# The recurrence's scaled input: one VectorE operation in place of two on GpSimd

## The chip, the cores and the metric

The kernel runs on one core of a Trainium2 chip. The metric is the device time of one execution, in microseconds (us). Five engines work side by side: TensorE (PE; its weight loads are listed apart, as PEld), VectorE (DVE), ScalarE (ACT), GpSimd (POOL) and SyncE (SP, which here only issues DMAs). Each takes its instructions in the order in which the program gives them, and an instruction that waits for a semaphore holds up everything behind it on its engine.

## The reference

The program is a decoder of two layers over 8 sequences of 256 tokens, 256 wide: windowed attention, cross-attention, experts; then a gated linear recurrence, cross-attention, a binarized feed-forward. Each sublayer is added to its input and normalized. The change lies in the recurrence alone:

```python
gi = jnp.einsum('btd,hd->bth', x, W_in)
gate, xc = jnp.split(gi, 2, axis=-1)
...                                   # causal convolution over time, 4 taps, per channel: y
xc = jnp.transpose(y, (0, 2, 1))
g = jnp.einsum('bth,gh->btg', xc, W_g) + b_g
forget, inp = jnp.split(g, 2, axis=-1)
alpha = jnp.exp(ALPHA_LOG_SCALE * jax.nn.softplus(forget_base) * jax.nn.sigmoid(forget))
beta = jnp.sqrt(1.0 - alpha ** 2 + 1e-06)
bterm = beta * jax.nn.sigmoid(inp) * xc
_, h = lax.associative_scan(_scan_combine, (alpha, bterm), axis=1)
out = jnp.einsum('bth,dh->btd', jax.nn.gelu(gate, approximate=False) * h, W_out)
```

A sigmoid is computed as half of one plus a tanh. So `sigmoid(inp) * xc` is, up to the factor one half (which is taken into beta), tanh plus one, times the convolution: the scaled input.

## The kernel before

The sublayers run one after another as blocks. In the recurrence the work goes by batch (one sequence of 256 tokens); hidden channels stand on the partitions, 512 channels as four tiles of 128, and the tiles are taken in two pairs, p = 0 and 1, so most operations on a pair are 128 partitions by 512 elements (two tiles of 256 tokens). The work is written by hand as a software pipeline over three batches; `both` (L1985) runs `batch(b)` for b = 0 to 7, of which 1 to 4 in a hardware loop. In `batch(b)` each engine does, in this order:

- PE: for b+1 the transposes of the tokens (L2246) and the projection in (`way_in`, L2255); the gate projections of b for tiles 0 and 1 (L2267); the projection out of b-1 (`way_out`, L2275); the gate projections of tiles 2 and 3.
- ACT: the transposed tokens of b+1 to SBUF (`re_xt`, L2084), the convolution's input (`re_padded`, L2091), the roots beta of b-1 (L2119), the Gelu gates of b+1 (L2098, which wait until b-1 is gated), and per tile of b two tanh (`re_tf` L2105, `re_ti` L2108), a third tanh and an exponential (`re_T` L2112, `re_E` L2113). `re_ti` is the tanh of the input gate.
- DVE: half of the convolution of b+1 (L2168, L2171), the entry of b+2 (the expert output added to the tokens, its statistics), scan and gating of b-1 for both pairs (`re_h` L2187, `re_gh` L2191), the other half of the convolution, the normalization of b+2, residual and statistics of b-1 (L2196), then `decay(b, 0)` (`re_d` L2178, `re_nb` L2180, `re_alpha` L2181), the layer norm of b-1 (L159), `decay(b, 1)`.
- POOL: the gather of expert rows for b+3 (`fetch`, an indirect DMA, L2030), beta times scaled input of b-1 for both pairs (`re_bterm`, L2051), the inverse roots for two norms (L155), and then `scale_input(b, 0)` and `scale_input(b, 1)`: two operations each, L2043 (tanh times convolution) and L2045 (plus convolution).

`re_bterm` is what the scan waits for, the scan releases the gating, the gating releases `way_out` and the ACT gates.

Of the kernel before, what the change touches and what calls it, by code (L numbers as in the profile page):

```python
# [23 lines left out]
ALU = mybir.AluOpType  # L24
# [80 lines left out]
def at(ap, index):  # L105

    return ap[:, index] if isinstance(index, int) else ap[:, bass.ds(index, 1)].squeeze(1)
# [55 lines left out]
def first(b):  # L163

    return isinstance(b, int) and b == 0
# [22 lines left out]
    first=([("project", n) for n in range(6)] + [("turn", 0), ("turn", 1), ("project", 6), ("turn", 2), ("turn", 3)]  # L188
           + [("project", n) for n in range(7, 12)] + [("turn", n) for n in range(4, 8)]),
# [14 lines left out]
def window_attention(nc, x_dram, xt_dram, wqkv_dram, wo_dram, rope_dram, ident, half, X, next_loads):  # L204
# [522 lines left out]
    first=[("key", 0), ("value", 0), ("tokens", 0), ("query", 0)],  # L727
# [1122 lines left out]
HT = HID // P  # L1850
# [68 lines left out]
def recurrence(nc, gates, slots, slot, ident, half, X, next_loads):  # L1919


    with ExitStack() as ctx:
        def sb(name, shape, dt=F32):
            return ctx.enter_context(nc.sbuf_tensor("re_" + name, shape, dt))

        def sem(name):
            return ctx.enter_context(nc.semaphore("re_" + name))
# [10 lines left out]
        conv = [sb(f"conv{k}", [P, HT, SEQ]) for k in range(2)]  # L1938
        gate = [sb(f"gate{k}", [P, HT, SEQ]) for k in range(2)]
        tf = sb("tf", [P, 2, SEQ])  # L1940
        ti = [sb(f"ti{p}", [P, 2, SEQ]) for p in range(2)]
# [6 lines left out]
        scaled = [sb(f"scaled{p}", [P, 2, SEQ]) for p in range(2)]  # L1948
# [24 lines left out]
        ti_done = sem("ti_done")  # L1973
        T_done = sem("T_done")
        chain = sem("chain")
        beta_ready = sem("beta_ready")
        doubled = sem("doubled")
        scaled_ready = sem("scaled_ready")
        bterm_ready = sem("bterm_ready")
        scanned = sem("scanned")  # L1980
# [32 lines left out]
        @block.gpsimd  # L2013
        def _(pool):
            pool.memset(tiny[:], 0.25e-6).then_inc(consts, 1)

            def fetch(b, par):

                def passes(n):

                    pool.tensor_tensor(carry[:, 2 * par + n:2 * par + n + 1], half[:], half[:], ALU.add)

                if not (isinstance(b, int) and b < 2):
                    pool.wait_ge(entered, (b - 1) * TPB)
                    passes(0)
                pool.tensor_copy(where[par][:], slot[:, bass.ds(b * TPB, TPB)]).then_inc(pointed, 1)
                pool.wait_ge(pointed, b + 1)
                passes(1)
                for t in range(TPB):
                    pool.indirect_dma_start(out=y[par][:, t], out_offset=None, in_=slots.rows[:, :],  # L2030
                                            in_offset=bass.IndirectOffsetOnAxis(ap=where[par][:, t:t + 1], axis=0)).then_inc(gathered[par], 16)

            def root_in(b):
                norm_in.root(pool, b, 0)
                norm_in.root(pool, b, 1)

            def scale_input(b, par, p):

                c = conv[par][:, 2 * p:2 * p + 2]
                pool.wait_ge(ti_done, b * HT + 2 * p + 2)  # L2040
                if not first(b):
                    pool.wait_ge(bterm_ready, 2 * b + p - 1)
                pool.tensor_tensor(scaled[p][:], ti[p][:], c, ALU.mult).then_inc(doubled, 1)  # L2043
                pool.wait_ge(doubled, 2 * b + p + 1)
                pool.tensor_tensor(scaled[p][:], scaled[p][:], c, ALU.add).then_inc(scaled_ready, 1)  # L2045

            def times_beta(b, p):

                pool.wait_ge(scaled_ready, 2 * b + p + 1)
                pool.wait_ge(beta_ready, 2 * b + p + 1)  # L2050
                pool.tensor_tensor(bterm[p][:], scaled[p][:], beta[p][:], ALU.mult).then_inc(bterm_ready, 1)  # L2051

            def batch(b, par, before=True, after=True, enters=True, fetches=True):
                if fetches:
                    fetch(b + 3, 1 - par)
                if before:
                    times_beta(b - 1, 0)
                    times_beta(b - 1, 1)
                if enters:
                    root_in(b + 2)  # L2060
                if before:
                    norm.root(pool, b - 1, 0)
                    norm.root(pool, b - 1, 1)
                scale_input(b, par, 0)
                scale_input(b, par, 1)

            for b in (0, 1):
                fetch(b, b)
            root_in(0)
            root_in(1)  # L2070
            fetch(2, 0)
            both(batch)(pool)
            times_beta(BATCH - 1, 0)
            times_beta(BATCH - 1, 1)
            norm.root(pool, BATCH - 1, 0)
            norm.root(pool, BATCH - 1, 1)
# [64 lines left out]
        def _(dve):  # L2141
# [12 lines left out]
            def enter_norm(b):  # L2154
                for t in range(TPB):
                    norm_in.apply(dve, b, t, at(X, b * TPB + t))

            def convolve(b, par, p):
# [4 lines left out]
                for tap in range(TAPS):  # L2163
                    for k in range(2):
# [6 lines left out]
                            ins = dve.scalar_tensor_tensor(out=out, in0=x, scalar=w, in1=out, op0=ALU.mult, op1=ALU.add)  # L2171
                        ins.then_inc(conved, 1)

            def decay(b, p):

                n = 6 * b + 3 * p
                dve.wait_ge(T_done, b * HT + 2 * p + 2)
                dve.scalar_tensor_tensor(out=d[p][:], in0=E[p][:], scalar=1.0, in1=T[p][:], op0=ALU.add, op1=ALU.mult).then_inc(chain, 1)  # L2178
                dve.wait_ge(chain, n + 1)
                dve.scalar_tensor_tensor(out=nb[p][:], in0=d[p][:], scalar=-2.0, in1=d[p][:], op0=ALU.add, op1=ALU.mult).then_inc(chain, 1)  # L2180
                dve.tensor_scalar(alpha[p][:], d[p][:], -1.0, 1.0, ALU.mult, ALU.add).then_inc(chain, 1)  # L2181
# [11 lines left out]
            def residual(b):  # L2193
                dve.wait_ge(out_done, b + 1)
                for t in range(TPB):
                    dve.tensor_tensor(norm.res[:, t], o_bank[:, t], at(X, b * TPB + t), ALU.add).then_inc(summed, 1)  # L2196
                    dve.wait_ge(summed, b * TPB + t + 1)
                    norm.statistics(dve, b, t)

            def layer_norm(b):  # L2200
                for t in range(TPB):
                    norm.apply(dve, b, t, at(X, b * TPB + t))

            def batch(b, par, before=True, after=True, enters=True, fetches=True):
                if after:
                    convolve(b + 1, 1 - par, 0)
                if enters:
                    enter(b + 2, par)
                if before:
                    scan(b - 1, 1 - par, 0)  # L2210
                    scan(b - 1, 1 - par, 1)
                if after:
                    convolve(b + 1, 1 - par, 1)
                if enters:
                    enter_norm(b + 2)
                if before:
                    residual(b - 1)
                decay(b, 0)
                if before:
                    layer_norm(b - 1)  # L2220
                decay(b, 1)

            for b in (0, 1):
# [475 lines left out]
```

## Time and profile before

| | us |
|---|---|
| runs | 1460.71, 1465.9, 2265.28; median 1465.9 |
| profiled execution | 1460.69 |
| its span | 1459.0 |
| PE busy in the span | 1213.4 (83%) |
| DVE busy | 1056.3 (72%) |
| ACT busy | 724.3 (50%) |
| POOL busy | 429.4 (29%) |
| the recurrence, first transposes to last norm | 948.7 to 1189.8 |

The span is the time between the first and the last instruction in the profile; the device time beside it is 1.7 us longer. Busy times are shares of the whole span and mean little for one stage. A timeline's start is counted from the start of the span.

### The profile page before, as it was taken

The page shows a single profiled execution, that of the slowest core. Times are in us where ns is not written, and L with a number is a line of the kernel's source. Part 1 is how long each engine was busy: PE and PEld are TensorE (multiplying, and loading weights), DVE is VectorE, ACT ScalarE, POOL GpSimd, SP SyncE. Part 2 cuts the span into 40 slices and gives each one's busy share as a digit, 9 for nine tenths or more (in the row PEclk, how much of TensorE's full clock was granted, in tenths as well). Part 3 has the DMA queues.
Part 4 walks back from the last instruction along what each step waited for, and adds up shares of the span by engine and source line. Part 5 has one row for each costly group of instructions (what it writes and reads, how often), then busy time and mean ns, then how long its engine had stood idle before and what let it go on. Part 6 is the DMA issues. An engine that isn't in the chain of part 4 may idle for free. (4 is left out here: it accounts for less than half of the span.)

```text
span 1459.0 us, 28684 instructions
## 1 busy us (share of the span) xinstructions
PE 1213.4 (83%) x9867; PEld 967.3 (66%) x9867; DVE 1056.3 (72%) x2303; ACT 724.3 (50%) x1442; POOL 429.4 (29%) x478
## 2 busy tenths in 40 slices
PE   4789897998889878999632999499989849998687
PEld 1477676677667866777531777378878737777575
DVE  5587777786777854888583876358887737888588
ACT  3454544454444423555361777345555515655184
POOL 4212020211202013555203000125453334555223
PEclk8899999999999997999755999789999969999699
DMA  5000000010000004000223451120000020000011
GB/s 198 8 2 9 9 1 10 1 62 1 3 2 1 2 7 163 18 17 17 110 117 127 152 210 53 58 83 22 22 15 8 0 82 11 20 19 8 29 44 44
DMA packets 33924, 64.35 MB, mean 44 GB/s; under 512 B 7574, under 2 KB 23446, under 8 KB 30742
## 3 DMA queue, kind: packets, MB, share of 16 engines
q1 hardware_dynamic: 32278, 58.70, 11.4%
q0 software_dynamic: 1536, 4.20, 0.9%
q8 instruction: 67, 1.10, 0.3%
q14 instruction: 43, 0.35, 0.1%
HBM read 42.12 MB, written 12.39 MB: 37 GB/s over the span
## 5 line engine op out<-in xcount | busy, mean ns | idle before, releaser
L345 POOL TENSOR_TENSOR wa_rot<-wa_raw,wa_cos_sin 128x1024 f32<-128x1024 f32 x32 | 80.5, 2517 | 347.3 <-ACT wa_raw L389 344.9
L891 POOL TENSOR_TENSOR ca_z<-ca_z,ca_top 128x308 f32<-128x308 f32 x128 | 92.7, 724 | 136.5 <-DVE ca_top L1020 136.2
L639 PE MATMUL wa_scores<-wa_kt,wa_qt 128*128 128x192 f32 x512 | 119.4, 345 | 0.0
L2267 PE MATMUL re_g<-re_conv,re_w_g 128*128 128x256 f32 x512 | 112.8, 379 | 0.0
L963 ACT ACTIVATE ca_pth<-ca_turned 77x512 f16<-77x512 f32 x128 | 75.8, 592 | 61.4 <-PE ca_turned L1147 60.7
L2267 PEld LDWEIGHTS re_g<-re_conv,re_w_g 128*128 128x128 f32 x512 | 97.3, 190 | 13.2
L1147 PE MATMUL ca_turned<-ident,ca_probs 128*77 128x128 f32 x512 | 85.0, 290 | 19.4 <-ACT ca_probs L955 18.4
L1138 PE MATMUL ca_scores<-ca_km,ca_q 128*128 128x308 f32 x256 | 92.1, 444 | 5.9 <-ACT ca_q L936 5.7
L605 PE MATMUL wa_shared<-wa_wh,wa_xh 128*128 128x512 f16 x192 | 75.8, 395 | 18.6 <-DVE wa_wl L453 9.3
L1025 DVE SCALAR_TENSOR_TENSOR ca_ptl<-ca_turned,ca_pth 77x512 f16<-77x512 f32 x128 | 86.7, 677 | 2.6 <-ACT ca_pth L963 2.6
L639 PEld LDWEIGHTS wa_scores<-wa_kt,wa_qt 128*128 128x128 f32 x512 | 78.8, 194 | 12.9 <-issue 0.7
L389 ACT ACTIVATE wa_raw<-wa_shared 128x512 f32<-128x512 f32 x64 | 38.1, 597 | 95.2 <-PE wa_shared L605 95.2
L526 DVE SCALAR_TENSOR_TENSOR wa_ptl<-wa_turned,wa_pth 128x384 f16<-128x384 f32 x128 | 65.8, 551 | 23.8 <-ACT wa_pth L430 22.5
L955 ACT ACTIVATE ca_probs<-ca_z 128x308 f32<-128x308 f32 x128 | 58.2, 455 | 44.5 <-POOL ca_z L891 43.5
L468 DVE TENSOR_TENSOR wa_sine<-wa_raw,wa_cos_sin 128x512 f32<-128x512 f32 x64 | 63.6, 1035 | 22.7 <-ACT wa_raw L389 13.2
L613 PE MATMUL wa_shared<-ident,wa_rot 128*128 128x128 f32 x256 | 42.9, 301 | 42.3 <-DVE wa_vl L480 37.5
L503 DVE TENSOR_REDUCE wa_top<-wa_scores 128x2 f32<-128x384 f32 x128 | 70.3, 549 | 8.1 <-PE wa_scores L639 7.7
L605 PE MATMUL wa_shared<-wa_wl,wa_xh 128*128 128x512 f16 x192 | 75.6, 394 | 0.0
L605 PE MATMUL wa_shared<-wa_wh,wa_xl 128*128 128x512 f16 x192 | 75.3, 392 | 0.0
L505 DVE TENSOR_TENSOR wa_shifted<-wa_scores,wa_top 128x384 f32<-128x384 f32 x128 | 71.4, 558 | 4.4
L1147 PEld LDWEIGHTS ca_turned<-ident,ca_probs 128*77 128x77 f32 x512 | 56.7, 150 | 25.6 <-ACT ca_probs L955 21.8
L2255 PE MATMUL re_in<-re_xt,re_w_in 128*128 128x256 f32 x256 | 62.0, 404 | 13.5 <-ACT re_xt L2084 13.5
(315 smaller groups left out, 3700.0 us busy)
## 6 DMA issues: line engine op xcount, KB each, us to landing
ex_stage<-in_ew SPq DMA_DIRECT2D x16, 1024.0 KB, 6.8
slots<-slots_zeros SPq DMA_DIRECT2D x10, 512.0 KB, 5.9
ca_xs<-tokens SPq DMA_DIRECT2D x16, 256.0 KB, 2.4
ex_xe<-slots SPq DMA_DIRECT2D x11, 320.0 KB, 3.2
wa_w_stage<-in_wqkv SPq DMA_DIRECT2D x6, 512.0 KB, 4.4
slots<-ex_y SPq DMA_DIRECT2D x9, 320.0 KB
wa_x_stage<-in_xt SPq DMA_DIRECT2D x8, 256.0 KB, 3.0
tokens<-in_x SPq DMA_DIRECT2D x1, 2048.0 KB, 10.4
```

What stands on the lines that cost most here:

```text
L345: pool.tensor_tensor(rot[:, r % 2], raw[:, r % 2], c, ALU.mult).then_inc(cos_done, 1)
L503: dve.tensor_reduce(top[:, k], s_bank[t][:, :, 0:SPAN], AX.X, ALU.max).then_inc(maxed, 1)
L505: dve.tensor_tensor(shifted[k][:], s_bank[t][:, :, 0:SPAN], top[:, k].unsqueeze(2).broadcast_to((P, 2, SPAN)), ALU.subtract).then_inc(shif ...
L526: dve.scalar_tensor_tensor(out=windows(ptl[k][:]), in0=windows(t_bank[h][:]), scalar=PSCALE, in1=windows(pth[k][:]), op0=ALU.mult, op1=ALU ...
L605: ins = pe.matmul(dst[:], a[:, par, k, tok], w[:, k, cols], start=(k == 0 and n == 0), stop=(k == KT_ - 1 and n == 2))
L639: ins = pe.matmul(dst, qt[par][:, 2 * u + h, t * P:(t + 1) * P], kt[par][:, u, t * WINDOW:t * WINDOW + SPAN], start=False, stop=True)
L891: pool.tensor_tensor(z[k][:], z[k][:], top[:, k].unsqueeze(2).broadcast_to((P, UH, CTX)), ALU.subtract).then_inc(shift, 1)
L963: act.activation(pth[k][0:CTX], t_bank[k][0:CTX], ACT.Copy, scale=PSCALE).then_inc(probs_high, 1)
L1025: dve.scalar_tensor_tensor(out=ptl[k][0:CTX], in0=t_bank[k][0:CTX], scalar=PSCALE, in1=pth[k][0:CTX], op0=ALU.mult, op1=ALU.subtract).then ...
L1138: pe.matmul(s_bank[c % 2][:, 0:UH * CTX], q[par][:, g, t * P:(t + 1) * P], km[par][:, g, h:h + UH].rearrange("p h k -> p (h k)"), start=Tr ...
L1147: ins = pe.transpose(t_bank[k][0:CTX, h * P:(h + 1) * P], probs[k][:, h], ident[:])
L2267: ins = pe.matmul(g_bank[m][:, k], w_g[:, j, cols], conv[par][:, j], start=(j == 0), stop=(j == HT - 1))
```

## The change

`scale_input` moves from GpSimd's program to VectorE's and becomes one operation: (ti + 1) * conv. On GpSimd it was the last thing in a batch, for both pairs. On VectorE it stands ahead of `decay(b, p)`, once for each pair. Its waits are the same two: for `ti` of its pair, and that `re_bterm` of the batch before has been made of the buffer. The semaphore between the two GpSimd operations goes.

```diff
-            def scale_input(b, par, p):
-
-                c = conv[par][:, 2 * p:2 * p + 2]
-                pool.wait_ge(ti_done, b * HT + 2 * p + 2)
-                if not first(b):
-                    pool.wait_ge(bterm_ready, 2 * b + p - 1)
-                pool.tensor_tensor(scaled[p][:], ti[p][:], c, ALU.mult).then_inc(doubled, 1)
-                pool.wait_ge(doubled, 2 * b + p + 1)
-                pool.tensor_tensor(scaled[p][:], scaled[p][:], c, ALU.add).then_inc(scaled_ready, 1)
...
                     norm.root(pool, b - 1, 1)
-                scale_input(b, par, 0)
-                scale_input(b, par, 1)
...
+            def scale_input(b, par, p):
+
+                dve.wait_ge(ti_done, b * HT + 2 * p + 2)
+                if not first(b):
+                    dve.wait_ge(bterm_ready, 2 * b + p - 1)
+                dve.scalar_tensor_tensor(out=scaled[p][:], in0=ti[p][:], scalar=1.0, in1=conv[par][:, 2 * p:2 * p + 2],
+                                         op0=ALU.add, op1=ALU.mult).then_inc(scaled_ready, 1)
...
                     residual(b - 1)
+                scale_input(b, par, 0)
                 decay(b, 0)
                 if before:
                     layer_norm(b - 1)
+                scale_input(b, par, 1)
                 decay(b, 1)
```

VectorE in the hardware loop, from the residual's last statistic to the next batch's convolution, before (`re_d`, `re_nb` and `re_alpha` are the decay, `tokens` the layer norm of the batch before):

```order
L150 TENSOR_SCALAR re_var_eps<-re_mv 128x1
L2177 ISA
L2178 SCALAR_TENSOR_TENSOR re_d<-re_E,re_T 128x512
L2179 ISA
L2180 SCALAR_TENSOR_TENSOR re_nb<-re_d 128x512
L2181 TENSOR_SCALAR re_alpha<-re_d 128x512
L159 TENSOR_SCALAR tokens<-re_res,re_mv,re_rstd 128x256 x2
L2177 REGISTER_ALU
L2178 SCALAR_TENSOR_TENSOR re_d<-re_E,re_T 128x512
L2179 REGISTER_ALU
L2180 SCALAR_TENSOR_TENSOR re_nb<-re_d 128x512
L2181 TENSOR_SCALAR re_alpha<-re_d 128x512
```

and the same stretch now:

```order
L150 TENSOR_SCALAR re_var_eps<-re_mv 128x1
L2163 ISA
L2165 ISA
L2166 SCALAR_TENSOR_TENSOR re_scaled<-re_ti,re_conv 128x512
L2173 SCALAR_TENSOR_TENSOR re_d<-re_E,re_T 128x512
L2174 ISA
L2175 SCALAR_TENSOR_TENSOR re_nb<-re_d 128x512
L2176 TENSOR_SCALAR re_alpha<-re_d 128x512
L159 TENSOR_SCALAR tokens<-re_res,re_mv,re_rstd 128x256 x2
L2163 REGISTER_ALU
L2166 SCALAR_TENSOR_TENSOR re_scaled<-re_ti,re_conv 128x512
L2173 SCALAR_TENSOR_TENSOR re_d<-re_E,re_T 128x512
```

One operation has come in ahead of each `re_d`; nothing else has changed its place.

GpSimd behind the loop, batches 5 to 7, before:

```order
L2051 TENSOR_TENSOR re_bterm<-re_scaled,re_beta 128x512 x2
L155 TENSOR_TENSOR re_rstd<-re_var_eps,half 128x1 x2
L2043 TENSOR_TENSOR re_scaled<-re_ti,re_conv 128x512
L2045 TENSOR_TENSOR re_scaled<-re_scaled,re_conv 128x512
L2043 TENSOR_TENSOR re_scaled<-re_ti,re_conv 128x512
L2045 TENSOR_TENSOR re_scaled<-re_scaled,re_conv 128x512
L2051 TENSOR_TENSOR re_bterm<-re_scaled,re_beta 128x512 x2
```

and now:

```order
L2040 TENSOR_TENSOR re_bterm<-re_scaled,re_beta 128x512 x2
L155 TENSOR_TENSOR re_rstd<-re_var_eps,half 128x1 x2
L2040 TENSOR_TENSOR re_bterm<-re_scaled,re_beta 128x512 x2
L155 TENSOR_TENSOR re_rstd<-re_var_eps,half 128x1 x2
```

The four operations between the inverse roots and the next `re_bterm` are gone, so `re_bterm` follows at once when its inputs are there. In the loop the gather `re_y` follows the inverse roots instead.

## Rows read from the trace of the kernel before

**Rows 1.** Busy time of each engine: one loop batch, and a later stretch.
```profile
1036.45:1063.35 26.90, 24.87 (x117) 21.70 (x116) 22.98 (x53) 15.09 (x26) 14.20 (x15) 1.00 0.06 19
...
1092.81:1101.50 8.69, 8.69 (x32) 7.33 (x33) 6.61 (x17) 3.81 (x5) 1.97 (x2) 0.80 0.00 0
```

**Rows 2.** Timeline of PE in the loop: start, length, instructions, idle before and its releaser.
```profile
1036.45 0.60 PE L2246 MATMUL re_x<-ident,re_xs 128*128 128x128 f32 x4
1039.08 7.17 PE L2255 MATMUL re_in<-re_xt,re_w_in 128*128 128x256 f32 x32 [2.03 <-ACT re_xt L2084]
...
1052.99 3.62 PE L2275 MATMUL re_out<-re_w_out,re_gh 128*128 128x256 f32 x16
```

**Rows 3.** Timeline of ACT in the same batch.
```profile
1036.65 0.47 ACT L2105 ACTIVATE re_tf<-re_g,re_half_bias 128x256 f32<-128x256 f32 x1 [1.64 <-PE re_g L2267]
...
1038.36 0.59 ACT L2084 ACTIVATE re_xt<-re_x 128x512 f32<-128x512 f32 x1
...
1052.25 1.28 ACT L2098 ACT_TABLE_LOAD   x1 [6.17 <-DVE re_gh L2191]
...
1060.10 0.47 ACT L2105 ACTIVATE re_tf<-re_g,re_half_bias 128x256 f32<-128x256 f32 x1 [0.66 <-PE re_g L2267]
```

**Rows 4.** Timeline of DVE in the loop: the two decays, first convolution.
```profile
1032.48 0.69 DVE L2178 SCALAR_TENSOR_TENSOR re_d<-re_E,re_T 128x512 f32<-128x512 f32 x1
1033.20 0.69 DVE L2180 SCALAR_TENSOR_TENSOR re_nb<-re_d 128x512 f32<-128x512 f32 x1
...
1061.77 1.49 DVE L2181 TENSOR_SCALAR re_alpha<-re_d 128x512 f32<-128x512 f32 x1
...
1065.40 0.88 DVE L2178 SCALAR_TENSOR_TENSOR re_d<-re_E,re_T 128x512 f32<-128x512 f32 x1 [1.49 <-ACT re_E L2113]
1066.32 1.64 DVE L2180 SCALAR_TENSOR_TENSOR re_nb<-re_d 128x512 f32<-128x512 f32 x1
1067.88 0.41 DVE L2181 TENSOR_SCALAR re_alpha<-re_d 128x512 f32<-128x512 f32 x1
1068.73 0.74 DVE L2168 TENSOR_SCALAR re_conv<-re_padded,re_hid 128x256 f32<-128x256 f32 x2 [0.44 <-ACT re_padded L2091]
```

**Rows 5.** Timeline of POOL in the loop.
```profile
1041.87 1.07 POOL L2030 DMA_INDIRECT re_y<-slots,re_where  x1 [0.16 <-issue]
...
1059.40 0.55 POOL L155 TENSOR_TENSOR re_rstd<-re_var_eps,half 128x1 f32<-128x1 f32 x1 [0.72 <-DVE re_var_eps L150]
```

**Rows 6.** The instructions of the tile re_scaled: duration in ns, min/median/max.
```profile
L2043 POOL TENSOR_TENSOR re_scaled<-re_ti,re_conv x16: 1265/1271/1479, 976.9 to 1169.8; 128x512 f32<-128x512 f32 x16
L2045 POOL TENSOR_TENSOR re_scaled<-re_scaled,re_conv x16: 1325/1590/1600, 978.2 to 1171.2; 128x512 f32<-128x512 f32 x16
```

**Rows 7.** Timeline of DVE behind the loop, around the scans of batch 6.
```profile
1150.14 1.49 DVE L2181 TENSOR_SCALAR re_alpha<-re_d 128x512 f32<-128x512 f32 x1
1151.55 2.33 DVE L2187 TENSOR_TENSOR_SCAN re_h<-re_alpha,re_bterm 128x256 f32<-128x256 f32 x2
...
1154.53 1.26 DVE L2187 TENSOR_TENSOR_SCAN re_h<-re_alpha,re_bterm 128x256 f32<-128x256 f32 x2
```

**Rows 8.** Timeline of POOL behind the loop.
```profile
1127.86 2.49 POOL L2051 TENSOR_TENSOR re_bterm<-re_scaled,re_beta 128x512 f32<-128x512 f32 x2 [5.03 <-ACT re_beta L2119]
...
1149.79 2.97 POOL L2051 TENSOR_TENSOR re_bterm<-re_scaled,re_beta 128x512 f32<-128x512 f32 x2
...
1172.91 2.94 POOL L2051 TENSOR_TENSOR re_bterm<-re_scaled,re_beta 128x512 f32<-128x512 f32 x2
```

**Rows 9.** Timeline of ACT behind the loop: the first root of batches 6 and 7.
```profile
1148.92 0.72 ACT L2119 ACTIVATE re_beta<-re_nb,re_tiny 128x512 f32<-128x512 f32 x1
...
1172.05 0.72 ACT L2119 ACTIVATE re_beta<-re_nb,re_tiny 128x512 f32<-128x512 f32 x1
```

**Rows 10.** Timeline of PE behind the loop: the last two projections out.
```profile
1156.57 5.41 PE L2275 MATMUL re_out<-re_w_out,re_gh 128*128 128x256 f32 x16 [3.90 <-DVE re_gh L2191]
...
1179.67 6.43 PE L2275 MATMUL re_out<-re_w_out,re_gh 128*128 128x256 f32 x16 [10.78 <-DVE re_gh L2191]
```

More of the change, by code:

```diff
@@ L1976, in recurrence @@
         beta_ready = sem("beta_ready")
-        doubled = sem("doubled")
         scaled_ready = sem("scaled_ready")
```

## The prediction

> **What bounds the kernel now.** The change touches one stage, so the busy shares of the whole program say little; I first took the busy times batch by batch inside the recurrence. A loop batch takes 26.90 us, PE is busy for 24.87 of them and DVE for 22.98 (the third and the first busy number of the row) [rows 1]. Then the timeline of PE. It runs through the whole batch with one gap: 2.03 us ahead of the projection in, which waits for ACT's copy `re_xt` [rows 2]. What sets that gap is in the timeline of ACT: PE ends the last gate tile, ACT wakes from its wait for it at 1036.65, does the four activations of that tile, and only then, at 1038.36, copies the tokens that PE transposed meanwhile [rows 3]. The gap is thus a loop between PE and ACT alone. GpSimd and VectorE are in it only if they make ACT or PE late.
>
> How late they may be shows in the same two views. The gating on DVE releases ACT at 1052.25, and PE takes up the projection out, which needs the same gating, at 1052.99: DVE could be about 0.7 us later there before PE stood still [rows 2, 3]. ACT, once released, is behind its work and catches up: it waits 0.66 us for PE ahead of tile 2, and some 1.6 us ahead of tile 3, so 2.3 us of lateness are made up before `re_xt` is touched [rows 3]. Ahead of that gating DVE stands idle twice: 1.49 us for `re_E` before the second decay, and 0.44 us for the convolution's input [rows 4]. DVE is busy, but it walks behind PE.
>
> Behind the loop it is different. In batches 6 and 7 PE runs out of other work and waits 3.90 and 10.78 us for the gating [rows 10]. There the path is: tanh, scaled input, `re_bterm`, scan, gating, projection out. These two places are the only ones where I expect the time to move.
>
> **The change part by part.**
>
> *Removed from GpSimd.* Sixteen pairs (two per batch, eight batches) of 1.27 and 1.59 us, 46 us in all [rows 6]. In the loop this engine's results are wanted late: `re_bterm` there is held by beta, not by the scaled input, and beta comes from ACT behind the convolution's input, which is set by PE. So the removal by itself is worth nothing to the loop.
>
> *Added to VectorE.* Sixteen operations of the same kind, shape and number of inputs as `re_d`, which takes 0.69 us when undisturbed [rows 4]: 11.0 us in all, 1.38 per batch. The trace has no such operation on `re_ti` and `re_conv`; the lower bound is 0.69, the upper is `re_nb`, also of this kind, beside a GpSimd operation, 1.64 [rows 4]. I take 0.69, since GpSimd's large operations that stood beside it are those removed.
>
> *Given back on VectorE.* `re_nb` takes 0.69 us at one place and 1.64 at another, `re_alpha` 0.41 and 1.49 [rows 4]; the long ones lie beside GpSimd's two scaled-input operations. Taking in a batch both `re_nb` as long and one `re_alpha`, what disappears is 0.95 + 0.95 + 1.08 = 3.0 us, against 1.38 added. DVE's load in a batch goes down by about 1.6 us, from 23.0 to 21.4. The Trainium skill ("SBUF — State Buffer", Who interferes with whom) says that a VectorE instruction with two inputs in SBUF and a GpSimd instruction that reads SBUF shut each other out for a whole instruction; by that rule the trace's two lengths are one operation, waiting or not.
>
> *Where they stand.* For pair 1, `re_ti` is ready two activations ahead of `re_E` (1.0 us at some 0.5 each), and DVE idles there for 1.49 us: the 0.69 us fit wholly into that wait. Without that cover they would reach the convolution, with 0.44 us more of idle, and then the 0.7 us at the gating. For pair 0 there is no wait ahead of `re_d`, so the first decay starts 0.69 later; `re_nb` and `re_alpha` behind it then cost up to 2.0 less, and the wait for `re_E` of pair 1 catches what is left. Loop and batch 0: 0 us.
>
> *The gather* on GpSimd now follows the inverse roots at once, at least the 5.7 us sooner that the two removed pairs took. Its rows are used more than a batch later; 0 us. Its issue takes 1.07 us beside the convolution's operations [rows 5].
>
> *The inverse roots* (0.55 us each [rows 5]) may meet the new operation of pair 0; the worst is that one waits for the other, 0.55 or 0.69 us, under the same cover; 0.
>
> *Batch 6, behind the loop.* Before, `re_bterm` started at 1149.79 after GpSimd's scaled input, while its other input, beta, was there at 1148.92 + 0.72 = 1149.64 [rows 8, 9]. So the start can come forward by 0.1 us only: ACT's root is next in line. But the pair of them took 2.97 us beside DVE's long operations and takes 2.49 undisturbed [rows 8], and `re_nb`, `re_alpha` on DVE are then done early. The end of the pair comes 0.1 + 0.4 us sooner, and the first scan, which lies beside GpSimd's second product and takes 2.33 us where an undisturbed pair takes 1.26 [rows 7], ends with it. Gain 0.45 us. Bounds: 0 (scan and product only change places) and 1.1 (the scan is not shut out at all, 2.33 against 1.26).
>
> *Batch 7.* The same: root ready at 1172.77, product at 1172.91, 2.94 us for the pair [rows 8, 9]. Gain 0.45, bounds 0 and 1.1.
>
> *Sum.* 0 + 0.45 + 0.45 = 0.9 us, bounds 0 and 2.2. The profiled execution took 1460.7 us (its span, 1459.0, and 1.7 around it); minus 0.9 is 1459.8. That execution agrees with one of the runs shown, the median is that of another, 5.2 us above; I keep to the profile's level.
>
> **The rivals.**
>
> *1. VectorE becomes the bound (slower).* It is at 85% in the loop, and the change gives it more instructions. If the new operations were not covered, and the long ones beside them did not shrink, the gating would come late by 1.38 us in seven batches, beyond the cover: 9.7 us, 1470.4. It decides from the point where what is added per batch exceeds the idle of 1.49 + 0.44 and the 0.7 at the gating, together 2.6 us [rows 2 to 4]. Even two operations at the upper price, 3.3 us, are only just beyond that, and pair 0's has the shrinking of `re_nb` for it. The page "Perfetto Trace Analysis" of the Trainium skill (Optimizing Scalar/DVE Operations) speaks for this rival: where VectorE is saturated it advises to move work off it, towards ScalarE or even GpSimd, and this change does the reverse. The trace bears that out only if VectorE's idle stretches are not where the new work falls. Chance 0.07.
>
> *2. The loop gets shorter (faster).* If DVE, not the loop of PE and ACT, held the batch, its 1.6 us less would come out in seven batches: 11.2 us, 1449.5. Against it: PE's only gap in a batch is released by `re_xt`, and ACT's chain ahead of that by PE. Chance 0.05.
>
> *3. The clock.* In one stretch of the same work, 1092.81 to 1101.50, the granted clock was 0.80 [rows 1], and a projection in took 8.7 us in place of 7.17; the projections out after PE's idle took 5.41 and 6.43 us against 3.62 in the loop [rows 2, 10]. If a dip falls away, or the shorter idle keeps the clock at its level for batch 6, 1.5 to 3.3 us more are won: 1456.5 to 1458.3; if a dip is added, 1.5 are lost: 1461.3. Chance 0.13, of both signs.
>
> *4. The gain is all eaten* because product and scan meet in the other order: 1460.7. Chance 0.13.
>
> **How the numbers follow.** The forecast, a loop that doesn't move and up to 1.1 us at each of two places, has 0.62; with rivals 3 and 4, which lie within 4 us of it, 0.88. The range takes these in, from 1455 (2.2 us at the tail and 3.3 of clock), and on the other side the 5.2 us by which runs of the same program differ, to 1466. What is left out is half of rivals 1 and 2. A measurement of this kernel can tell about 2%, 29 us, from no change. The whole recurrence is 240 us, and no case reaches 29 us: 0.01 faster, 0.98 within, 0.01 slower.
>
> **What would show it.** In the profile after: `re_scaled` on DVE at 0.69 us x16; both `re_nb` and `re_alpha` at 0.7 and 0.4 in nearly all batches; loop batches still of 26.9 us with the same gap of 2.0 us before the projection in; DVE's wait for `re_E` of pair 1 gone or shorter; PE's waits for the gating in batches 6 and 7 shorter by about half a microsecond each. A loop batch that isn't 26.9 us at the full clock would prove me wrong: then the gap on PE was not closed between PE and ACT alone.

## The result, and the profile after

| us | before | after |
|---|---|---|
| median of the runs (11 each) | 1460.38 | 1454.32 |
| their spread | 1455.99 to 1464.28, and one of 2265.28 | 1450.05 to 1459.03 |
| profiled execution | 1460.69 | 1450.05 |
| its span | 1459.0 | 1448.3 |
| DVE busy in the span | 1056.3 | 1040.3 |
| POOL busy in the span | 429.4 | 382.7 |

The ratio of after to before is 0.9962, with a 95% interval of 0.9944 to 0.9979. That is 5.5 us faster (3.1 to 8.2 us), and within 2%. The long run of before stands alone in both kernels' runs and is in no comparison. The forecast was 1459.8, with a range from 1455 to 1466: the kernel came out 5.5 us below the forecast and 0.7 us below the range.

The loop first. Busy times in one loop batch of the changed kernel, from one group of token transposes to the next (start and end, length, then busy us and instructions of PE, PEld, DVE, ACT and POOL, the granted clock, DMA share, GB/s), then PE's timeline in it:

```profile
1033.04:1059.94 26.90, 24.87 (x118) 21.71 (x116) 21.21 (x54) 15.09 (x26) 8.56 (x12) 1.00 0.05 19
```

```profile
1035.67 7.17 PE L2252 MATMUL re_in<-re_xt,re_w_in 128*128 128x256 f32 x32 [2.03 <-ACT re_xt L2071]
...
1049.58 3.62 PE L2272 MATMUL re_out<-re_w_out,re_gh 128*128 128x256 f32 x16
```

The batch takes 26.90 us as before, with the same gap of 2.03 us before the projection in [rows 1, 2]. DVE, which took on an operation per pair, is busy for less: 21.21 us against 22.98. GpSimd goes from 14.20 to 8.56.

What DVE does there now (timeline; start, length, idle before it and its releaser in brackets), and the instructions of three tiles over the whole execution (duration in ns, min/median/max):

```profile
1034.11 0.69 DVE L2166 SCALAR_TENSOR_TENSOR re_scaled<-re_ti,re_conv 128x512 f32<-128x512 f32 x1 [2.16 <-ACT re_ti L2095]
1035.08 0.69 DVE L2173 SCALAR_TENSOR_TENSOR re_d<-re_E,re_T 128x512 f32<-128x512 f32 x1 [0.28 <-ACT re_E L2100]
1035.81 0.69 DVE L2175 SCALAR_TENSOR_TENSOR re_nb<-re_d 128x512 f32<-128x512 f32 x1
1036.42 0.42 DVE L2176 TENSOR_SCALAR re_alpha<-re_d 128x512 f32<-128x512 f32 x1
1038.43 0.74 DVE L2155 TENSOR_SCALAR re_conv<-re_padded,re_hid 128x256 f32<-128x256 f32 x2 [1.59 <-ACT re_padded L2078]
```

```profile
L2166 DVE SCALAR_TENSOR_TENSOR re_scaled<-re_ti,re_conv x16: 691/692/694, 973.4 to 1164.2; 128x512 f32<-128x512 f32 x16
L2175 DVE SCALAR_TENSOR_TENSOR re_nb<-re_d x16: 691/691/693, 975.1 to 1165.9; 128x512 f32<-128x512 f32 x16
L2176 DVE TENSOR_SCALAR re_alpha<-re_d x16: 417/420/422, 975.7 to 1166.5; 128x512 f32<-128x512 f32 x16
```

Every `re_nb` is at 0.69 us and every `re_alpha` at 0.42; before they were at 1.64 and 1.49 beside GpSimd's operations [rows 4]. The wait of pair 1 has moved ahead of the new operation, and the convolution now has 1.59 us of idle before it where it had 0.44. DVE is further from holding PE up than it was before.

Behind the loop, the last two projections out, which before took 5.41 and 6.43 us after 3.90 and 10.78 us of idle [rows 10]. Timeline of PE in after:

```profile
1152.69 3.72 PE L2272 MATMUL re_out<-re_w_out,re_gh 128*128 128x256 f32 x16 [3.43 <-DVE re_gh L2186]
...
1173.64 6.08 PE L2272 MATMUL re_out<-re_w_out,re_gh 128*128 128x256 f32 x16 [10.33 <-DVE re_gh L2186]
```

Busy times and granted clock (the third number from the end of a row) over these two projections in after:

```profile
1152.69:1156.25 3.56, 3.56 (x17) 3.15 (x18) 0.00 (x0) 0.00 (x0) 0.00 (x0) 1.00 0.00 0
1173.64:1179.72 6.08, 6.08 (x16) 4.63 (x16) 0.00 (x0) 0.00 (x0) 0.00 (x0) 0.60 0.00 0
```

The same for before: the second half of its wait in batch 6, then batch 6's projection in three pieces of 1.8 us, then batch 7's whole:

```profile
1154.62:1156.57 1.95, 0.00 (x0) 0.00 (x0) 1.86 (x3) 1.18 (x3) 0.00 (x0) 1.00 0.00 0
1156.57:1158.37 1.80, 1.80 (x7) 1.59 (x8) 0.00 (x0) 0.00 (x0) 0.00 (x0) 0.87 0.00 0
1158.37:1160.17 1.80, 1.80 (x5) 1.36 (x5) 0.00 (x0) 0.00 (x0) 0.00 (x0) 0.50 0.00 0
1160.17:1161.97 1.80, 1.80 (x7) 1.54 (x6) 0.00 (x0) 0.00 (x0) 0.00 (x0) 0.69 0.00 0
...
1179.67:1186.10 6.43, 6.43 (x16) 4.90 (x16) 0.00 (x0) 0.00 (x0) 0.00 (x0) 0.57 0.00 0
```

The waits are 0.47 and 0.45 us shorter. More than that was saved in the work after them. Batch 6's projection takes 3.72 us at a granted clock of 1.00, the 2.4 GHz level, where it took 5.41: 1.69 us for 0.47 of waiting. In before the clock was still at 1.00 at the end of the wait, fell to the 1.2 GHz level (0.50) while PE was already at the projection, and came back before it ended. In after it did not fall. Batch 7's projection takes 0.35 less, at 0.60 against 0.57.

The dip of [rows 1], where a projection in took 8.7 us at a clock of 0.80, is in the changed kernel too:

```profile
1089.39 8.86 PE L2252 MATMUL re_in<-re_xt,re_w_in 128*128 128x256 f32 x32 [1.95 <-ACT re_xt L2071]
```

Every execution profiled of the two kernels has one such slow projection in, which costs 1.7 us, in batch 5 or in batch 6. It is no part of the difference.

Measured from PE's first matmul of a stage to its first of the next, in both profiled executions and in the further profiles of the same two kernels (us; the three stages not listed differ by 1.1 us at most between all of these):

| | window attention | recurrence | second cross-attention |
|---|---|---|---|
| before, five profiles | 537.8 to 541.9 | 244.6 to 244.8 | 171.4, 171.4, 171.3, 166.5, 166.6 |
| after, four profiles | 535.3 to 540.1 | 241.5 to 241.9 | 166.6, 166.6, 166.6, 168.9 |

The recurrence is 3.0 us shorter, with no overlap between the profiles. The first stage, whose code is untouched, differs by 4 to 5 us between profiles of one kernel. The third column is taken up under the experiments.

### The profile page after: what moved, and what is told of

The parts are those of the page before. It is cut to its first block and busy times, and to the rows that moved or that the text cites. A ratio compares the mean times of both kernels' runs of the same rounds, so it can differ in the third digit from the quotient of the medians.

```text
span 1448.3 us, 28656 instructions
## 1 busy us (share of the span) xinstructions
PE 1203.2 (83%) x9867; PEld 960.0 (66%) x9867; DVE 1040.3 (72%) x2319; ACT 723.8 (50%) x1442; POOL 382.7 (26%) x446
```

## The experiments

Each is the kernel before or after with the edit shown. Times are medians in us; a ratio is against the kernel before on the same chip.

**The same kernels again.** `before_again` and `after_again` are the two kernels unchanged.

> The kernel before, unchanged, as a second program against itself. If the 5.5 us between the two medians are the change's own work, this gives a ratio of 1.000 with an interval of about 0.002 to either side, and its profile shows the last two projections out at 5.4 and 6.4 us and the time from the recurrence's first transpose to the next stage's first matmul at 244.8 us. If that difference is partly the scatter between executions, the stages outside the recurrence differ here by 3 us and more from the first profile, as they do between before and after (window attention 2.7 us, second cross-attention 4.8 us).

> The changed kernel again, on this chip, for a second profile and a ratio that shares its runs of before with the halves. Theory T: recurrence 241.9 us, third-last projection out at 3.62, second-last 3.7 and last 6.1 us, ratio 0.998 (2.9 us) if the rest of the 5.5 us was scatter. If something outside the recurrence is really faster, 0.996 and the second cross-attention again at 166.6 in place of 171.4 us.

Before: 1460.77, ratio 0.9999 (0.9988 to 1.0011). After: 1454.55, ratio 0.9960 (0.9943 to 0.9977), against 0.9962 at first. The size of the result repeats; it was no accident of one chip.

**Where it comes from: behind the loop or in it.** Both carry GpSimd's old `scale_input` beside the new one and choose by batch (the comments are notes for the reader):

```diff
+        def on_vector(b):
+            return isinstance(b, int) and b >= BATCH - 2      # tail_only; loop_only has its opposite
...
+                if not on_vector(b):
+                    scale_input(b, par, 0)                    # GpSimd, two operations
+                    scale_input(b, par, 1)
...
+                if on_vector(b):
+                    scale_input(b, par, 0)                    # VectorE, one operation; p = 1 likewise
```

> The scaled input on VectorE in batches 6 and 7 alone; in batches 0 to 5 GpSimd does it in two operations as before. Theory T (everything the change wins in the recurrence is won at the two waits behind the loop, by 0.47 + 0.45 us of shorter wait and 1.7 + 0.35 us of clock at the projections out): the recurrence takes 241.9 us, the ratio is that of the change, 0.996 to 0.998. Theory L (VectorE's lighter load in the loop counts as well): 243 us or more, ratio nearer to 1.

> The opposite half: on VectorE in batches 0 to 5, on GpSimd in batches 6 and 7 as before. Theory T: the loop batches stay at 26.90 us, the recurrence at 244.8 us, ratio 1.000. Theory L: under 244 us and a ratio below 0.999.

`tail_only` took 1457.62, ratio 0.9973 (0.9959 to 0.9987); `loop_only` 1459.74, ratio 0.9998 (0.9984 to 1.0013). Timeline of PE, the last two projections out, of `tail_only` and then of `loop_only`:

```profile
1156.60 3.72 PE L2292 MATMUL re_out<-re_w_out,re_gh 128*128 128x256 f32 x16 [3.45 <-DVE re_gh L2204]
1177.55 5.97 PE L2292 MATMUL re_out<-re_w_out,re_gh 128*128 128x256 f32 x16 [10.33 <-DVE re_gh L2204]
```

```profile
1157.25 5.41 PE L2292 MATMUL re_out<-re_w_out,re_gh 128*128 128x256 f32 x16 [3.90 <-DVE re_gh L2204]
1180.34 6.36 PE L2292 MATMUL re_out<-re_w_out,re_gh 128*128 128x256 f32 x16 [10.78 <-DVE re_gh L2204]
```

The first has the waits and lengths of after and a recurrence of 241.6 us, the second those of before and 244.6. So the change does nothing in batches 0 to 5, and the 3.0 us come from batches 6 and 7. By the medians, two batches give 3.9 us (1.9 to 6.0) and the whole change 5.5 to 5.8; the intervals overlap, so the medians don't show whether the loop's part adds anything.

**GpSimd's old work kept beside the new.** GpSimd still computes both products, into a tile that nobody reads, and their buffers are held for it:

```diff
+            def old_work(b, par, p):
+                c = conv[par][:, 2 * p:2 * p + 2]
+                pool.wait_ge(ti_done, b * HT + 2 * p + 2)
+                ...
+                pool.tensor_tensor(unused[:], ti[p][:], c, ALU.mult).then_inc(doubled, 1)
+                ...
+                pool.tensor_tensor(unused[:], unused[:], c, ALU.add).then_inc(doubled, 1)
```

> The changed kernel, but GpSimd still does its two old operations at their old place, into a tile nobody reads. VectorE has the added work and not the relief. If the relief is what keeps VectorE in time, loop batches grow beyond 26.90 us (rival 1, up to 1470). If the cover by idle time is enough, as I think, the loop stays at 26.90 us and only the two places behind it suffer: there the new operation waits for GpSimd's product (up to 1.3 us) and the recurrence takes 245 to 247 us, ratio 1.000 to 1.002.

It took 1458.65, ratio 0.9997 (0.9984 to 1.0010): no gain in the median. Timeline of DVE in a loop batch, then PE's last two projections out:

```profile
1058.55 1.65 DVE L2191 SCALAR_TENSOR_TENSOR re_nb<-re_d 128x512 f32<-128x512 f32 x1
1060.11 1.49 DVE L2192 TENSOR_SCALAR re_alpha<-re_d 128x512 f32<-128x512 f32 x1
...
1064.64 1.64 DVE L2191 SCALAR_TENSOR_TENSOR re_nb<-re_d 128x512 f32<-128x512 f32 x1
1066.21 0.41 DVE L2192 TENSOR_SCALAR re_alpha<-re_d 128x512 f32<-128x512 f32 x1
1066.64 0.74 DVE L2171 TENSOR_SCALAR re_conv<-re_padded,re_hid 128x256 f32<-128x256 f32 x2
```

```profile
1154.90 5.41 PE L2288 MATMUL re_out<-re_w_out,re_gh 128*128 128x256 f32 x16 [4.41 <-DVE re_gh L2202]
...
1178.50 5.63 PE L2288 MATMUL re_out<-re_w_out,re_gh 128*128 128x256 f32 x16 [11.29 <-DVE re_gh L2202]
```

The long `re_nb` and `re_alpha` are back, at the very lengths they had before [rows 4], and it was GpSimd's two operations that made them so. The convolution has no idle left before it, yet the loop batch is still 26.90 us wherever the clock is at 1.00. The waits are 0.5 us longer than before, and the projection out of batch 6 is back at 5.41. The recurrence took 247.7 us, 2.9 more than before and a little above the 245 to 247 expected. The waits have 1.0 of these. The rest is the clock at other places: three projections in took 8.8 to 8.9 us in place of 7.17, where before has one (two loop batches were 28.57 us long by it, at a clock of 0.94), which adds 3.4 us; the very first projection in and the last one out were 0.7 and 0.8 us shorter. So the sum says little about the edit here, and the lengths say more.

**VectorE loaded further.** Two or four more operations of the same form, into an unread tile, ahead of each new one (four or eight per batch):

```diff
+                for i in range(2):                             # dve_plus4: range(4)
+                    ...
+                    dve.scalar_tensor_tensor(out=unused[:], in0=ti[p][:], scalar=1.0, in1=conv[par][:, 2 * p:2 * p + 2],
+                                             op0=ALU.add, op1=ALU.mult).then_inc(spare, 1)
```

> The changed kernel with two more copies of the new operation ahead of each one, into a tile nobody reads: 4 more per batch, about 2.8 us more of VectorE. If VectorE only walks behind PE, the idle of 2.2, 0.3 and 1.6 us that the profile of the change shows ahead of its second half covers them: loop batches 26.90 us, the recurrence longer by at most 0.3 us at each of the two last waits, ratio to before 0.996 to 0.998. If VectorE holds the batch, the loop grows by 2.8 us in each of 6 batches: 17 us.

> The changed kernel with four more copies of the new operation ahead of each one, results not read: 8 more per batch, 5.3 us of VectorE. VectorE's work per batch, 21.4 + 5.3 us with its one wait for the projection out of 1.0, is then above the 26.9 us of PE's batch: the loop must grow, by my count to 27.5 to 28.5 us a batch. If it stays at 26.90, the load of VectorE is still not what holds the batch; if it grows by the full 5.3 us, there was no cover at all.

`dve_plus2` took 1459.16, ratio 1.0000 (0.9982 to 1.0018), where 0.996 to 0.998 was expected; `dve_plus4` ran once, at 1461.43. Busy times of a loop batch of each, and PE's timeline: of `dve_plus2` the last two projections out, of `dve_plus4` a projection in and out of the loop and the last two out:

```profile
1039.59:1066.49 26.90, 24.87 (x116) 21.70 (x117) 23.75 (x59) 15.10 (x26) 8.43 (x11) 1.00 0.06 20
```

```profile
1156.89 3.72 PE L2279 MATMUL re_out<-re_w_out,re_gh 128*128 128x256 f32 x16 [3.71 <-DVE re_gh L2193]
1178.12 5.75 PE L2279 MATMUL re_out<-re_w_out,re_gh 128*128 128x256 f32 x16 [10.61 <-DVE re_gh L2193]
```

```profile
1013.08:1040.24 27.16, 25.14 (x116) 21.61 (x117) 26.02 (x63) 15.07 (x26) 10.24 (x11) 1.00 0.06 20
```

```profile
1013.08 7.17 PE L2259 MATMUL re_in<-re_xt,re_w_in 128*128 128x256 f32 x32 [2.03 <-ACT re_xt L2073]
...
1027.15 3.72 PE L2279 MATMUL re_out<-re_w_out,re_gh 128*128 128x256 f32 x16
...
1158.37 5.53 PE L2279 MATMUL re_out<-re_w_out,re_gh 128*128 128x256 f32 x16 [5.35 <-DVE re_gh L2193]
...
1183.06 5.14 PE L2279 MATMUL re_out<-re_w_out,re_gh 128*128 128x256 f32 x16 [12.25 <-DVE re_gh L2193]
```

This measures the cover. With 2.8 us more per batch than the change (4 times 0.7) the loop does not move; with 5.6 us more it goes to 27.2 or 27.3 in three batches of four, less than the 27.5 to 28.5 expected. DVE is busy for 26.02 of the 27.16, and the projection out takes 3.72 us where it took 3.62. So VectorE begins to hold the batch at between 2.8 and 5.6 us beyond the change, and the change is far from it. (DVE's busy time rose by less than the operations put in, by 2.54 and 4.81 us.) The second thing is in the tail: `dve_plus2` waits 3.71 us and still has the 3.72 of after, where before waited 3.90 and had 5.41. So the length of the wait decides, and not what the change did to the work. `dve_plus2` also holds a warning. Its recurrence took 242.1 us, 2.7 less than before, and its median is no shorter than before's. The other stages, whose code is the same, made up for all of it.

**The idle filled: is it the clock?** PE is kept at work in its waits with matrix products whose output nobody reads, ahead of the last two projections out, behind the last, and ahead of the cross-attention's first products. First too many of them:

```diff
+            def spin(par, n):
+                for i in range(n):
+                    pe.matmul(x_bank[:, 0], w_g[:, 0, 0:P], conv[par][:, 0], start=True, stop=True)
...
+                if not after:          # in the last batch alone
+                    spin(par, 13)      # ahead of way_out(6); the fitted kernels have 7
...
+                spin(1, 40)            # ahead of way_out(7); fitted 22
                 way_out(BATCH - 1)
+                spin(1, 14)            # behind it; fitted 7
...                                     # and 12 (fitted 6) in the next cross-attention
```

> The kernel before with idle-time matmuls on TensorE whose results nobody reads: 13 ahead of the projection out of batch 6, 40 ahead of that of batch 7, 14 behind it, and 12 at the start of the second cross-attention (0.22 us each at the full clock). Purpose: take the clock out of the comparison. Theory C (of the 5.5 us between before and after some 0.9 us is VectorE's and GpSimd's shorter path, the rest is clock: at the two projections out and at the start of the next stage): both projections out take 3.6 us here, the clock is up from the first matmuls of the cross-attention, and the time falls from 1461 to about 1451. Theory W (work, not clock): time as before, since the waits are the same.

> The same added matmuls in the changed kernel. Theory C: only 0.9 to 1.0 us less than the kernel before with the same matmuls, about 1450; the recurrence's two waits for the gating are shorter by 0.45 us each and all else is alike. Theory W: 5.5 us less than it.

1464.59, ratio 1.0028 (1.0016 to 1.0039), and 1463.87, ratio 1.0022 (1.0009 to 1.0034). About 1451 and 1450 were expected. The filler was twice as long as meant, since each product is recorded as two matmuls of 0.22 us: the 40 products took 17.43 us for a wait of 10.8. It now sets the time itself. Both projections out took 3.62 us with no idle before them in both kernels, and the difference between the two kernels is gone (to the next stage's first product that is read, 252.2 and 252.4 us). With the right number:

> The kernel before with fewer idle-time matmuls, sized to fit inside TensorE's waits (each of them is two passes of 0.22 us, so the 13, 40, 14 and 12 of the run before were twice too long and set the time themselves): 7 ahead of the projection out of batch 6, 22 ahead of that of batch 7, 7 behind it, 6 at the start of the second cross-attention. Nobody reads their results. Theory C (clock): the projections out take 3.6 us in place of 5.41 and 6.4, the recurrence 240.2 us in place of 244.8, the cross-attention's start is fast, ratio to before 0.993 to 0.995. Theory W (work): ratio 1.000.

> The same fitted matmuls in the changed kernel. Theory C: 0.9 us less than the kernel before with the same matmuls (recurrence 239.3 us against 240.2), ratio to before 0.992 to 0.994, so that what was left of the 5.5 us, beyond 0.9, was clock; this would also be faster than both kernels of the case. Theory W: 5.5 us less than the kernel before with the same matmuls.

1451.41, ratio 0.9936 (0.9915 to 0.9957), and 1451.35, ratio 0.9942 (0.9921 to 0.9962). Timeline of PE, of the kernel before with filler, and of the kernel after with filler:

```profile
1158.79 3.72 PE L2283 MATMUL re_out<-re_w_out,re_gh 128*128 128x256 f32 x16 [0.89 <-DVE re_gh L2194]
1169.25 9.66 PE L2276 MATMUL re_x<-re_conv,re_w_g 128*128 128x256 f32 x44
1180.22 3.72 PE L2283 MATMUL re_out<-re_w_out,re_gh 128*128 128x256 f32 x16 [1.31 <-DVE re_gh L2194]
```

```profile
1156.48 3.72 PE L2280 MATMUL re_out<-re_w_out,re_gh 128*128 128x256 f32 x16 [0.41 <-DVE re_gh L2189]
1166.94 9.66 PE L2273 MATMUL re_x<-re_conv,re_w_g 128*128 128x256 f32 x44
1177.44 3.72 PE L2280 MATMUL re_out<-re_w_out,re_gh 128*128 128x256 f32 x16 [0.84 <-DVE re_gh L2189]
```

At the full clock the two kernels differ only in their waits, 0.89 against 0.41 and 1.31 against 0.84: 0.95 us. Up to the next stage's first product that is read, their recurrences are 240.5 and 239.7 us, 0.8 apart, with 2.7 us of filler in that stage counted in. That is what the change is worth as work, and it is the forecast's 0.9. The other 2.0 to 2.2 us of the 3.0 were the clock's: 1.69 and 0.35 in the two projections, and what is left is within the scatter of the profiles. These two also have the lowest medians of all, about 9 us under the kernel before (6 to 12). Whether they beat the change itself was not measured side by side; the intervals of the ratios (0.9915 to 0.9957, and 0.9944 to 0.9979 for the change) overlap by a little. With the filler in, the medians no longer tell whether the change is there.

**What of the rest?** The recurrence explains 3.0 of 5.5 us. The two kernels again, run and profiled once each:

> The kernel before once more, for the second cross-attention: it took 171.4 us in both profiles of before so far and 166.6 in both of the change, though nothing in it differs. If that is the program, 171.4 again. If it is where the clock's rise falls in its first 20 us by chance, some other value between 164 and 172 turns up.

> The changed kernel once more, for the places where the clock is granted. The projections out behind the loop 3.7 and 6.0 to 6.1 us and the recurrence 241.6 to 241.9 us, as in both profiles so far, since these hang on the length of the waits. The second cross-attention 166.6 again, or one of the longer values (up to 171.4): both are possible if its first 20 us are a matter of chance, and a value over 168 would show it for this kernel too.

> As for the third look at the changed kernel: recurrence 241.6 to 241.9 us; second cross-attention open between 166 and 172.

> The kernel before, fourth look: recurrence 244.6 to 244.8 us with projections out of 5.41 and 6.4 us; second cross-attention 171.4 (two looks) or 166.5 (one look) or between.

> The kernel before, fifth look: recurrence 244.6 to 244.8 us with projections out of 5.41 and 6.4 us; second cross-attention open between 166 and 172.

They took 1459.39, 1453.92, 1456.35, 1459.20 and 1459.76. The recurrence kept to its two lengths in all of them. The second cross-attention has a long and a short form, and they part at one place. Timeline of PE at its start, of before and then of after; then busy times and clock from the stage's first product, in stretches of 5, 5 and 10 us of before and of after, and the second of these of `before_3`:

```profile
1198.80 3.67 PE L1107 MATMUL ca_shared<-ca_xt,ca_w 128*128 128x256 f32 x8 [0.78 <-ACT ca_xt L933]
```

```profile
1192.43 1.97 PE L1107 MATMUL ca_shared<-ca_xt,ca_w 128*128 128x256 f32 x8 [0.78 <-ACT ca_xt L933]
```

```profile
1193.50:1198.50 5.00, 4.52 (x16) 3.39 (x16) 0.42 (x1) 0.98 (x3) 2.19 (x2) 0.50 0.92 334
1198.50:1203.50 5.00, 3.77 (x9) 2.63 (x9) 0.00 (x0) 1.14 (x4) 0.21 (x1) 0.62 0.55 208
1203.50:1213.50 10.00, 8.17 (x41) 6.30 (x42) 4.95 (x11) 4.31 (x9) 2.10 (x3) 0.66 0.01 2
```

```profile
1187.13:1192.13 5.00, 4.52 (x16) 3.40 (x16) 0.42 (x1) 0.98 (x3) 2.19 (x2) 0.50 0.90 327
1192.13:1197.13 5.00, 3.27 (x12) 2.12 (x12) 1.37 (x4) 2.58 (x5) 0.21 (x1) 1.00 0.57 217
1197.13:1207.13 10.00, 7.50 (x77) 6.21 (x78) 7.34 (x17) 5.31 (x12) 4.90 (x7) 1.00 0.01 2
```

```profile
1201.40:1206.40 5.00, 3.27 (x12) 2.12 (x12) 1.42 (x4) 2.53 (x5) 0.16 (x1) 0.98 0.53 199
```

Before and after both start at the 1.2 GHz level (0.50), after the 7.4 us in which PE waits for the context. In `before_3` and in after the clock is at the 2.4 GHz level in the next stretch; in the first profile of before it is at 0.62, and at 0.66 in the one behind it, and the same eight matmuls take 3.67 us in place of 1.97. Before fell into the long form in three profiles of five, after into a middle one (168.9) in one of four. On average that is 2.3 us for the change (169.4 against 167.2). The first stage gives another 1.6 us (540.0 against 538.4), so with the recurrence's 3.0 the profiles come to 6.9 us. The other kernels have a say too. `loop_only`, `tail_only`, `pool_keeps`, `dve_plus2` and `dve_plus4` leave this stage as it is; it took 167.7, 168.2, 168.7, 169.1 and 170.0 us in them, each time with the short start of 1.97 us. So the long start was seen in before alone, but `loop_only`, whose last two batches are those of before, did not have it, and middle lengths come with either scaled input. In the two fitted kernels, with filler ahead of this start, the stage took 167.0 and 166.3 us from its first product that is read. That is too little to say that the change shifts the odds, and no run here set the moment of that stage's start by itself, so this part stays open; so do the 4 to 5 us by which the first stage differs between profiles of the same kernel.

## Why the prediction was right in the mechanism and wrong in the size

*What bounds the kernel:* right. The gap of 2.03 us, closed between PE and ACT, is the same in after, in `dve_plus2` and in `dve_plus4`, where VectorE was at 26.02 us of 27.16.

*Removed from GpSimd, nothing for the loop:* right; `loop_only` is at 0.9998 and its loop batches at 26.90.

*Added to VectorE, 0.69 us each:* right, 692 ns for the median of the sixteen.

*Given back on VectorE:* right in kind, and the load came out at 21.21 against a forecast of 21.4. `pool_keeps` shows the cause by putting it back: with GpSimd's operations there, `re_nb` is again at 1.65 and `re_alpha` at 1.49. By the Trainium skill ("SBUF — State Buffer", Who interferes with whom) a VectorE instruction with two SBUF inputs and a GpSimd instruction that reads SBUF shut each other out; this case's rows agree, with two lengths of one operation, 0.69 and 1.64. `re_alpha` has one tile as input and was lengthened too; the same section counts its form, a tensor-scalar, among those that can take the shared ports.

*The cover:* right, and more of it than I counted. I had put the point at which VectorE decides at 2.6 us per batch; with the load 1.6 us lower on top of that the idle should cover 4.2 us beyond the change. The loop held with 2.8 more, as it should, and with 5.6 more it gave 0.3 us where 1.4 were uncovered. Of the missing 1.1 us, 0.8 never reached VectorE's busy time, which rose by 4.81 only; the rest is cover that I did not find.

*Batches 6 and 7, 0.45 us each:* right as waits. They fell by 0.47 and 0.45. The path is in the timelines of POOL and of DVE in batch 6:

```profile
1146.37 2.50 POOL L2040 TENSOR_TENSOR re_bterm<-re_scaled,re_beta 128x512 f32<-128x512 f32 x2 [7.37 <-ACT re_beta L2106]
...
1167.34 2.48 POOL L2040 TENSOR_TENSOR re_bterm<-re_scaled,re_beta 128x512 f32<-128x512 f32 x2 [7.38 <-ACT re_beta L2106]
```

```profile
1147.67 2.33 DVE L2182 TENSOR_TENSOR_SCAN re_h<-re_alpha,re_bterm 128x256 f32<-128x256 f32 x2 [1.69 <-POOL re_bterm L2040]
...
1150.64 1.26 DVE L2182 TENSOR_TENSOR_SCAN re_h<-re_alpha,re_bterm 128x256 f32<-128x256 f32 x2
```

GpSimd is now released by the root, the pair of products takes 2.50 and 2.48 us where it took 2.97 and 2.94 [rows 8], and DVE stands idle for the product where it was still busy before. The first scan keeps its 2.33 us [rows 7], so product and scan still meet, as the forecast had it. The 0.1 us for an earlier start did not come: from the start of the gate projections ahead (1138.69 before, 1135.28 after) to GpSimd's first product it is 11.10 and 11.09 us. The whole 0.47 is the shorter pair of products.

*The step that failed is the sum, in its term for the clock.* It left the work of PE behind each wait at the length it had, and put the clock with rival 3, at 0.13, worth 1.5 to 3.3 us. The runs show that term in every profile of the changed kernel: 1.69 us in batch 6's projection and 0.35 in batch 7's, 2.0 in all, beside 0.9 of work. (For batch 7 the runs show the shorter length each time, but not what sets it.) The row to read was already there: 5.41 us after an idle of 3.90, where the same 16 matmuls take 3.62 without one [rows 2, 10]. A projection slower than in the loop but not twice as slow is one in which the clock fell on the way, and I read that row as a fixed price of the place instead of a price that hangs on the wait. The rival's other ways did not come: the dip of [rows 1] neither fell away nor was one added. With that term the forecast would have been 1457.8, 3.5 us above the 1454.3 that came. The level from which it was counted, 1460.7, was right: the median of all runs of before is 1460.38. The Trainium skill ("Perfetto Trace Analysis", Matmul Optimizations) says that the matrix engine scales its power with use and that products should come back to back in batches; the rows of before and after agree in part (a clock of 1.00 through the loop, 0.50 in the projection behind the wait). That advice does not cover the dip of [rows 1], ahead of which PE was busy for 24.87 us of every 26.90.

*The rest of the size.* Of 5.5 us, 3.0 are in the recurrence and shown. The other 2.5 are outside it, in stages whose code did not change, and no case of the prediction had them. What caused them stays open. Their interval reaches down to 0.1 (3.1 less 3.0). `dve_plus2`, at 242.1 us in the recurrence and no faster in the median, shows that such amounts come and go there. Without them the time would have been some 1457, inside the range.

*Rival 1,* VectorE as the bound: wrong; `dve_plus2` and `dve_plus4` stand on either side of the point where it would come true. The prediction gave half of what the Trainium skill says there ("Perfetto Trace Analysis", Optimizing Scalar/DVE Operations). The same paragraph adds that GpSimd and VectorE share an SBUF read port, so that moving work between those two might not help. This case agrees with that second half, and goes further: VectorE's busy time per batch fell by 1.77 us when it was given GpSimd's work. *Rival 2,* a shorter loop: wrong, 26.90. *Rival 4,* the gain eaten: wrong.

## What to carry to other kernels

- Where PE waits a few microseconds behind a loop, read the length of the work behind the wait and its granted clock, not the wait alone: if the same products take longer there than in the loop, a small change of the wait can be worth several times itself (here 0.47 us of wait and 1.69 of work). Filling the idle with unread products, sized to fit, took the kernel before to 0.9936 of its time without the change.
- Work can cost less on the busier of two engines, if on the other engine it lengthens the busier one's operations: two GpSimd operations of 1.27 and 1.59 us became one of 0.69 on VectorE, and its neighbours went from 1.64 to 0.69.
- Before crediting a difference of some microseconds to an edit, see that the stage with the edit has it. Stages with the same code differed by 4 to 5 us here between executions.

## What the runs showed of the hardware that was not expected

- Of the same 16 matmuls (128x256, f32, two for each product): 3.62 us without a wait, 3.72 after 3.43, 3.45 and 3.71 us of idle, 5.41 after 3.90 and 4.41, 5.53 after 5.35. After the long waits it was 6.43 after 10.78, 6.08 after 10.33, 5.75 after 10.61, 5.63 after 11.29 and 5.14 after 12.25. A longer idle did not make slower work there: those lengths don't follow the wait, and I have no rule for them.
- The clock also fell where PE had not waited for more than 2.03 us in four batches: in every profile of before and after, one projection in took 8.86 us in place of 7.17, at 0.80 over its length, in batch 5 or 6 (in before's first profile the clock was 0.59 over the first 4.2 us of it). `dve_plus4` had none of these, `after_hot` two and `pool_keeps` three.
- One float32 product of 128x128 by 128x256 is recorded as two matmuls of 0.22 us: 22 products make the row of x44 with 9.66 us.
- The second cross-attention starts from the same instructions and the same 7.4 us of waiting, and its clock was up in the second 5 us in some executions and still at 0.66, on the mean, 10 to 20 us in, in others: 5 us of difference, between profiles of the kernel before alone.
